# Moving one of three quantization passes over a weight tile from VectorE to ScalarE

## The chip, the cores and the metric

The kernel runs on all 8 cores of one Trainium2 chip. Each core works alone on its own rows: cores 2b and 2b+1 share batch b, and each owns every other block of 128 tokens of it, 2048 in all. The metric is the device time of one launch in microseconds, that of the slowest core, as a median over runs.

## The reference

One transformer layer in postnorm form on x of shape (4, 4096, 1024), float32: causal attention with 16 heads over a latent of 128, then a gated feed-forward block whose matrices and inputs are quantized.

```python
def _weight_quant(w):
    scale = 1.0 / jnp.clip(jnp.mean(jnp.abs(w)), 1e-05)
    wq = jnp.clip(jnp.round(w * scale), -1.0, 1.0) / scale
    return w + jax.lax.stop_gradient(wq - w)

def _act_quant(x):
    scale = 127.0 / jnp.clip(jnp.max(jnp.abs(x), axis=-1, keepdims=True), 1e-05)
    xq = jnp.clip(jnp.round(x * scale), -128.0, 127.0) / scale
    return x + jax.lax.stop_gradient(xq - x)

def _bitlinear(x, w):
    return jnp.einsum('bsi,oi->bso', _act_quant(x), _weight_quant(w))

# feed-forward: w_gate, w_up are (4096, 1024), w_down is (1024, 4096)
gate = jax.nn.silu(_bitlinear(x, w_gate))
up = _bitlinear(x, w_up)
ffn = _bitlinear(gate * up, w_down)

x = _layernorm(x + attention(x))
x = _layernorm(x + ffn(x))
```

What matters here is `_weight_quant`: each weight is multiplied by one scale, rounded, and clipped to -1, 0 or 1. The scale needs the mean over the whole matrix, so each matrix is read twice.

## The kernel before

Every instruction goes through `Prog.emit`, which appends it to the list of its engine with the semaphore counts that it waits for; each engine runs its list in that order. `set_auto` makes every VectorE, ScalarE and GpSimd instruction also wait for the one before it on its engine; DMAs are exempt from that. A DMA is issued by the engine on whose list it stands (SP, ScalarE or GpSimd), and it waits there for its own semaphores, so whatever stands behind it on that list waits as well.

The program has three blocks. The first computes keys, values and queries and, in between, quantizes the three feed-forward matrices; the second is attention with its output projection and layer norm; the third is the feed-forward block. The second and third are not touched.

In the first block a loop over `c5` (8 chunks of 512 tokens) transposes x (PE to PSUM, then copied out in turns by VectorE and ScalarE, L29 and L30), makes `kvT` (L396), and then runs 4 head groups `hc`. A head group is one long chain in which VectorE does nearly everything: L414 (copy out of PSUM) to L426, then `Ln` and `Exp` on ScalarE (L429, L432), then L435 to L492 on VectorE with short matmuls in between.

The quantization is a generator, `f0_emitter` (L260 to L331), of which `f0_step(n)` emits n steps at that place of every list. One step stands behind `kvT` and two behind each head group, nine in a chunk; `f0_step(200)` (L499) emits all that is left behind the last chunk. In the order of steps, for each of `wg` (8 tiles of 128x4096), `wu` (8 tiles of 128x4096) and `wd` (32 tiles of 128x1024):

- pass 1, one step a tile: load (L277), `Abs` with a row sum on ScalarE (L286), add on VectorE (L290);
- one step that turns the sum into the scale `sclw` (L294 to L300);
- pass 2, one step a tile: load (L310, DMA rows carry L311), then three instructions on VectorE: times scale plus MAGIC (L314, which rounds, MAGIC being 1.5*2^23), minus MAGIC and min 1 (L318), max -1 into bfloat16 (L322), then the store to DRAM (L325, L326).

There are two float32 buffers, `wfbuf[i % 2]`, but one bfloat16 buffer, since both entries of `wqbuf` are the same tile; so L322 waits until the store of the tile before has landed. Loads of even tiles are issued by SP, those of odd tiles by ScalarE. All stores are issued by SP, which makes its order: load of an even tile, its store, the store of the odd tile behind it, load of the next even tile. The load of tile i in pass 2 waits for the store of tile i-2:

```python
w = [(cV, mksc[1])]
if dmk[bi] is not None:
    w.append((qP[bi], dmk[bi][1]))
mkd = P.emit(y if bi == 0 else "scalar", ... dma_start(wfbuf[bi] <- src tile i), waits=w, ...)
```

By the counting of steps, pass 2 of `wg` has tile 0 behind `kvT` and then the pairs (1,2), (3,4), (5,6) behind head groups and tile 7 with the first tile of the next pass; pass 2 of `wu` has tiles 0 and 1 alone and then the pairs (2,3), (4,5), (6,7); pass 2 of `wd` has tile 0 alone, the pairs (1,2), (3,4), and the remaining 27 tiles (5 to 31) in one go with no other work between them: the drain.

Of the kernel before, what the change touches and what calls it, by code (L numbers as in the profile page):

```python
# [9 lines left out]
F32 = mybir.dt.float32  # L10
BF16 = mybir.dt.bfloat16
AF = mybir.ActivationFunctionType
ALU = mybir.AluOpType
# [76 lines left out]
def build_nc():  # L90
# [26 lines left out]
    with es:  # L117
# [17 lines left out]
        sclw = sb("sclw", [128, 1], F32)  # L135
        absacc = sb("absacc", [128, 1], F32)
        negMb = sb("negMb", [128, 1], F32)
        sm = sb("sm", [128, 16], F32)
        sm4 = sb("sm4", [4, 2048], F32)

# [16 lines left out]
        with at:  # L157
# [9 lines left out]
            with s1:  # L167
# [24 lines left out]
                with ps1:  # L192
# [15 lines left out]
                    def _gchain(fn):  # L208
                        global _unused
                        nonlocal _gprev  # L210
                        _gprev = P.emit(g, fn, waits=([_gprev] if _gprev else []), incs=[(cG, 1)])
                    _gchain(lambda e: e.memset(ident[:], 1.0))
                    _gchain(lambda e: e.affine_select(ident[:], ident[:], [[1, 128]], ALU.is_equal, 0.0, base=0, channel_multiplier=-1))
                    _gchain(lambda e: e.memset(mtmp[:], 1.0))
# [45 lines left out]
                    def f0_emitter():  # L260
                        dmk = [None, None]
                        for wi, (src, dst, nt, ncols) in enumerate(
                                [(dwg, sg, 8, INNER), (dwu, su, 8, INNER), (dwd, sd, 32, D)]
                                if STAGE >= 1 else []):
                            mk_z = P.emit(g, lambda e: e.memset(absacc[:], 0.0),
                                          waits=[(cV, cV.v)], incs=[(cG, 1)])
                            vmk = [None, None]
                            for i in range(nt):
                                bi = i % 2
                                w = [(cG, mk_z[1])] if i < 2 else []  # L270
                                if dmk[bi] is not None:
                                    w.append((qP[bi], dmk[bi][1]))
                                if vmk[bi] is not None:
                                    w.append((cV, vmk[bi][1]))
                                mkd = P.emit(y if bi == 0 else "scalar",
                                             lambda e, i=i, bi=bi, src=src, ncols=ncols:
                                             e.dma_start(out=wfbuf[bi][:, 0:ncols],  # L277
                                                         in_=src[i * 128:(i + 1) * 128, :]),
                                             waits=w, incs=[(qF[bi], 16)], dma=True)
                                wsm = [(qF[bi], mkd[1])]  # L280
                                wsm += [(qP[k], dmk[k][1]) for k in range(2) if dmk[k]]
                                if vmk[0] is not None:
                                    wsm.append(vmk[0])
                                if vmk[1] is not None:
                                    wsm.append(vmk[1])
                                mka = P.emit(s, lambda e, bi=bi, ncols=ncols: e.activation(  # L286
                                    wqbuf[bi][:, 0:ncols], wfbuf[bi][:, 0:ncols], AF.Abs,
                                    accum_out=sm[:, 0:1]), waits=wsm,
                                    incs=[(cA, 1)])
                                vmk[bi] = P.emit(v, lambda e: e.tensor_add(  # L290
                                    absacc[:], absacc[:], sm[:, 0:1]),
                                    waits=[(cA, mka[1])], incs=[(cV, 1)])
                                yield
                            mkmm = P.emit(t, lambda e: e.matmul(  # L294
                                ps_sw[:], onesf[:], absacc[:], start=True, stop=True),
                                waits=[(cV, cV.v)], incs=[(cT, 1)])
                            P.emit(v, lambda e, wi=wi: e.tensor_scalar(
                                swb[:, wi:wi + 1], ps_sw[:], 1.0 / float(INNER * D), 1e-5,
                                ALU.mult, ALU.max), waits=[(cT, mkmm[1])])
                            mksc = P.emit(v, lambda e, wi=wi: e.reciprocal(  # L300
                                sclw[:], swb[:, wi:wi + 1]), waits=[(cA, cA.v)],
                                incs=[(cV, 1)])
                            yield
                            for i in range(nt):
                                bi = i % 2
                                w = [(cV, mksc[1])]
                                if dmk[bi] is not None:
                                    w.append((qP[bi], dmk[bi][1]))
                                mkd = P.emit(y if bi == 0 else "scalar",
                                             lambda e, i=i, bi=bi, src=src, ncols=ncols:  # L310
                                             e.dma_start(out=wfbuf[bi][:, 0:ncols],  # L311
                                                         in_=src[i * 128:(i + 1) * 128, :]),
                                             waits=w, incs=[(qF[bi], 16)], dma=True)
                                P.emit(v, lambda e, bi=bi, ncols=ncols: e.tensor_scalar(  # L314
                                    wfbuf[bi][:, 0:ncols], wfbuf[bi][:, 0:ncols],
                                    sclw[:, 0:1], MAGIC, ALU.mult, ALU.add),
                                    waits=[(qF[bi], mkd[1])])
                                P.emit(v, lambda e, bi=bi, ncols=ncols: e.tensor_scalar(  # L318
                                    wfbuf[bi][:, 0:ncols], wfbuf[bi][:, 0:ncols],
                                    MAGIC, 1.0, ALU.subtract, ALU.min))  # L320
                                wv2 = [(qP[k], dmk[k][1]) for k in range(2) if dmk[k]]
                                vmq = P.emit(v, lambda e, bi=bi, ncols=ncols: e.tensor_scalar_max(  # L322
                                    wqbuf[bi][:, 0:ncols], wfbuf[bi][:, 0:ncols], -1.0),
                                    waits=wv2, incs=[(cV, 1)])
                                dmk[bi] = P.emit(y, lambda e, i=i, bi=bi, dst=dst, ncols=ncols:  # L325
                                                 e.dma_start(out=dst[i * 128:(i + 1) * 128, :],  # L326
                                                             in_=wqbuf[bi][:, 0:ncols]),
                                                 waits=[(cV, vmq[1])], incs=[(qP[bi], 16)])
                                yield
# [979 lines left out]
```

How the kernel before makes its waits and increments, by code:

```python
            def run(e):  # L74
                for fn, waits, incs in ops:
                    for h, v in waits:
                        e.wait_ge(h, v)
                    if fn is None:
                        assert not incs, "fn=None cannot carry incs"
                        continue
                    inst = fn(e)
                    for h, n in incs:
                        inst.then_inc(h, n)
```

## Time and profile before

| | us |
|---|---|
| median of 2 runs | 3676.5 (3674.17 to 3678.82) |
| the profiled execution | 3674.18 |
| span of its slowest core, core 0 | 3672.6 |
| spans of the 8 cores | 3645.8 to 3672.6 |
| mean granted TensorE clock of the cores | 0.635 to 0.694 of full speed |

| core 0, busy | us | share of the span |
|---|---|---|
| TensorE matmul | 1753.4 | 48% |
| VectorE | 1416.9 | 39% |
| ScalarE | 1014.3 | 28% |
| GpSimd | 18.8 | 1% |

| stage on core 0 | from, us | to, us |
|---|---|---|
| pass 2 of `wg`, between head groups | 163 | 326 |
| pass 2 of `wu`, between head groups | 445 | 572 |
| pass 2 of `wd`, tiles 0 to 4 | 894 | 950 |
| pass 2 of `wd`, the drain | 950 | 1083 |
| queries, attention, feed-forward | 1083 | 3673 |

A share of busy time is an average over stages with different limits; here each stage is read by itself. In the timeline a row is the start, the duration, the engine, the line, the operation, and in brackets how long the engine had been idle and what ended that. ACTq and SPq rows are DMA issues; several of one kind may be merged into one row ("x2").

### The profile page before, as it was taken

The numbers are of one execution on the slowest core, as the hardware profiler recorded it, in microseconds if no ns is written. First come the engines' busy times: TensorE is split into PE (matmuls) and PEld (weight loads), VectorE is DVE, ScalarE is ACT, GpSimd is POOL, SyncE is SP. The second block draws the span as 40 slices with busy tenths as digits, with TensorE's granted clock in tenths as the row PEclk, the third lists the DMA queues.
The fourth block names the chain that finished last, engine by engine and source line by source line (L and its number), as shares of the span: only waits on it lengthen the run. The fifth ranks groups of instructions, "written<-read, shape, count | busy, mean of one in ns | idle before, by whom it ended". The sixth has DMA issues, their size and how long they took to land.

```text
span 3672.6 us, 31765 instructions; the slowest of 8 cores (3645.8 to 3672.6 us)
## 1 busy us (share of the span) xinstructions
PE 1753.4 (48%) x8824; PEld 593.5 (16%) x8824; DVE 1416.9 (39%) x2757; ACT 1014.3 (28%) x1228; POOL 18.8 (1%) x54
## 2 busy tenths in 40 slices
PE   1201112222004443456577587719745862962874
PEld 0000000000001111111111111104312321421331
DVE  1453464444445554432321311144524524444352
ACT  1301301221000002457478488801201211120120
POOL 1000000000000000000000000000000000000000
PEclk9999555555555555555555555559977995986997
DMA  5445354221440000010100100033224223412522
GB/s 120 148 161 172 137 202 124 69 69 55 134 137 12 1 0 12 6 41 1 46 1 1 46 1 1 1 115 115 64 75 138 86 76 102 130 61 69 166 61 77
DMA packets 140977, 278.35 MB, mean 76 GB/s; under 512 B 7944, under 2 KB 106504, under 8 KB 134664
## 3 DMA queue, kind: packets, MB, share of 16 engines
q1 hardware_dynamic: 107256, 192.96, 15.9%
q10 hardware_dynamic: 24320, 67.12, 5.4%
q0 software_dynamic: 9232, 16.25, 2.8%
q8 instruction: 78, 1.28, 0.1%
q14 instruction: 91, 0.75, 0.1%
HBM read 250.61 MB, written 41.94 MB: 80 GB/s over the span
## 4 chain that ended last, share of the span: by engine, by line
PE 21%; ACT 16%; DVE 11%; DMA 7%; issue 4%; DVEq 1%; ACTq 0%; SPq 0%
PE ps_f L1063 6%; PE ps_f L1069 6%; PE ps_f L1177 5%; DMA wdbuf<-scr_d 4%; ACT PTb L730 4%; ACT PTb L734 4%; ACT PT L730 3%; ACT PT L734 3%; ACT hqT L30 2%; DMA xo_t<-xo 2%; DVE den_sb L808 1%; PE ps_sc L706 1%; DMA x1f<-scr_x 1%; DMA wubuf<-scr_u 1%; PE ps_den L761 1%
## 5 line engine op out<-in xcount | busy, mean ns | idle before, releaser
L706 PE MATMUL ps_sc<-qn,khat 32*128 32x512 bf16 (+3 forms) x1280 | 313.8, 531 | 136.3 <-ACT PT L730 50.1
L1177 PE MATMUL ps_f<-wdbuf,hqT 128*128 128x512 bf16 x1024 | 262.0, 406 | 97.2 <-DMA wdbuf<-scr_d 46.3
L1063 PE MATMUL ps_f<-wgbuf,xqT 128*128 128x512 bf16 x1024 | 248.6, 387 | 119.0 <-DMA wubuf<-scr_u 118.1
L1069 PE MATMUL ps_f<-wubuf,xqT 128*128 128x512 bf16 x1024 | 245.2, 383 | 0.0
L742 DVE TENSOR_TENSOR PT<-PT,maskD 128x512 bf16<-128x512 bf16 x64 | 27.2, 425 | 489.1 <-ACT PT L734 489.1
L1083 DVE SCALAR_TENSOR_TENSOR hbuf<-ps_f,xsc,gate_s 128x512 f32<-128x512 f32 x128 | 96.1, 751 | 273.5 <-ACT gate_s L1077 273.5
L730 ACT ACTIVATE PT<-ps_sc,negMb 128x1024 bf16<-128x1024 f32 (+3 forms) x160 | 157.8, 986 | 121.2 <-PE ps_sc L706 108.8
L1077 ACT ACTIVATE gate_s<-ps_f,xsc 128x512 f32<-128x512 f32 x128 | 88.0, 687 | 345.2 <-PE ps_f L1069 345.2
L353 PE MATMUL ps_tr<-ident,xst 128*128 128x128 bf16 x384 | 52.2, 304 | 268.0 <-DVE xTc L29 176.5
L286 ACT ACTIVATE wqbuf_s<-wfbuf 128x1024 bf16<-128x1024 f32 (+1 forms) x48 | 91.7, 1910 | 291.6 <-DVE absacc L290 127.7
L730 ACT ACTIVATE PTb<-ps_sc,negMb 128x1024 bf16<-128x1024 f32 (+3 forms) x160 | 157.8, 986 | 36.0 <-PE ps_sc L706 24.6
L734 ACT ACTIVATE PT<-ps_sc,negMb 128x1024 bf16<-128x1024 f32 (+3 forms) x160 | 157.8, 986 | 16.0 <-ACT PT L730 1.5
L734 ACT ACTIVATE PTb<-ps_sc,negMb 128x1024 bf16<-128x1024 f32 (+3 forms) x160 | 157.8, 986 | 14.8
L423 PE MATMUL ps_ss<-kr2buf,ind4T 128*4 128x512 bf16 x32 | 18.7, 585 | 298.8 <-DVE krall L418 298.8
L706 PEld LDWEIGHTS ps_sc<-qn,khat 32*128 32x128 bf16 x1280 | 69.5, 99 | 466.8 <-issue 465.5
L1063 PEld LDWEIGHTS ps_f<-wgbuf,xqT 128*128 128x128 bf16 x1024 | 101.1, 99 | 243.7 <-issue 127.4
L1177 PEld LDWEIGHTS ps_f<-wdbuf,hqT 128*128 128x128 bf16 x1024 | 98.0, 102 | 251.4 <-issue 170.5
L30 ACT COPY hqT<-ps_tf 128x512 bf16<-128x512 bf16 x128 | 75.1, 586 | 190.4 <-PE ps_tf L958 183.2
L429 ACT ACTIVATE sm<-sm 4x512 f32<-4x512 f32 x32 | 20.1, 628 | 376.4 <-DVE sm L426 376.4
L450 PE MATMUL ps_bc<-rkh,ind 4*128 4x512 bf16 x32 | 18.6, 580 | 217.3 <-DVE rkl L446 217.3
L1069 PEld LDWEIGHTS ps_f<-wubuf,xqT 128*128 128x128 bf16 x1024 | 101.3, 99 | 124.5 <-issue 6.6
L314 DVE TENSOR_SCALAR wfbuf<-wfbuf,sclw 128x1024 f32<-128x1024 f32 (+1 forms) x48 | 61.7, 1286 | 120.9 <-DMA wfbuf<-wdT 74.8
(223 smaller groups left out, 2403.2 us busy)
## 6 DMA issues: line engine op xcount, KB each, us to landing
wgbuf<-scr_g SPq DMA_DIRECT2D x32, 1024.0 KB, 5.5
wubuf<-scr_u SPq DMA_DIRECT2D x32, 1024.0 KB, 8.4
wfbuf<-wgT SPq DMA_DIRECT2D x8, 2048.0 KB, 10.5
wfbuf<-wgT ACTq DMA_DIRECT2D x8, 2048.0 KB, 9.1
wfbuf<-wuT SPq DMA_DIRECT2D x8, 2048.0 KB, 14.0
wfbuf<-wuT ACTq DMA_DIRECT2D x8, 2048.0 KB, 10.3
wfbuf<-wdT SPq DMA_DIRECT2D x32, 512.0 KB, 3.8
wfbuf<-wdT ACTq DMA_DIRECT2D x32, 512.0 KB, 3.9
```

Of the source, the lines that this page charges most:

```text
L30: return e.copy(dst, src)
L286: mka = P.emit(s, lambda e, bi=bi, ncols=ncols: e.activation(wqbuf[bi][:, 0:ncols], wfbuf[bi][:, 0:ncols], AF.Abs, accum_out=sm[:, 0:1]), ...
L314: P.emit(v, lambda e, bi=bi, ncols=ncols: e.tensor_scalar(wfbuf[bi][:, 0:ncols], wfbuf[bi][:, 0:ncols], sclw[:, 0:1], MAGIC, ALU.mult, ALU ...
L353: e.transpose(ps_tr[bank][:, i4 * 128:(i4 + 1) * 128], src, ident[:]),
L706: e.matmul(ps_sc[:, j * 512 + stc:j * 512 + 512], khat[32 * j:32 * j + 32, gi * T + sc * 128: gi * T + sc * 128 + 128], qn[32 * j:32 * j + 32,
L730: mk_expA = P.emit(s, lambda e, stc=stc, pp=pp: e.activation(PTr[pp][:, 0:2, stc:512], PSr[:, 0:2, stc:512], AF.Exp, bias=negMb[:, 0:1]), ...
L734: mk_exp = P.emit(s, lambda e, stc=stc, pp=pp: e.activation(PTr[pp][:, 2:4, stc:512], PSr[:, 2:4, stc:512], AF.Exp, bias=negMb[:, 0:1]), w ...
L1063: P.emit(t, lambda e, c=c, i4=i4, bi=bi, gb=gb: e.matmul(ps_f[:, gb:gb + 512], xqT[:, i4 * D + c * 128:i4 * D + c * 128 + 128], wgbuf[bi][ ...
L1069: P.emit(t, lambda e, c=c, i4=i4, bi=bi, ub=ub: e.matmul(ps_f[:, ub:ub + 512], xqT[:, i4 * D + c * 128:i4 * D + c * 128 + 128], wubuf[bi][ ...
L1077: e.activation(gate_s2[par][:], ps_f[:, gb:gb + 512], AF.Silu, scale=xsc[:, c8 + 3:c8 + 4]),
L1083: e.scalar_tensor_tensor(hbuf[:, i4 * INNER + io * 512: i4 * INNER + io * 512 + 512], ps_f[:, ub:ub + 512], xsc[:, c8 + 4:c8 + 5], gate_s2 ...
L1177: e.matmul(ps_f[:, ((2 + i4) % 4) * 512: ((2 + i4) % 4) * 512 + 512], hqT[:, i4 * INNER + io * 128: i4 * INNER + io * 128 + 128], wdbuf[bi ...
```

## The change

In pass 2 the multiplication by the scale and the addition of MAGIC become one `activation` with `AF.Identity` on ScalarE, in place on the float32 tile, with `sclw` as its scale and a new constant tile `magicc` as its bias, both read from a column of 128 values. VectorE keeps L318 and L322. The activation waits for the load; L318 waits for the activation. The load of tile i no longer waits for the store of tile i-2 but for L322 of that tile (for the first two tiles of a matrix the old wait stays). GpSimd sets `magicc` once at the start. The list of ScalarE in pass 2 becomes: activation of an even tile, load of the odd tile behind it, activation of that tile.

```diff
--- before.py
+++ after.py
@@ -135,6 +135,7 @@
         sclw = sb("sclw", [128, 1], F32)
         absacc = sb("absacc", [128, 1], F32)
         negMb = sb("negMb", [128, 1], F32)
+        magicc = sb("magicc", [128, 1], F32)
         sm = sb("sm", [128, 16], F32)
         sm4 = sb("sm4", [4, 2048], F32)
 
@@ -209,6 +210,7 @@
                         global _unused
                         nonlocal _gprev
                         _gprev = P.emit(g, fn, waits=([_gprev] if _gprev else []), incs=[(cG, 1)])
+                    _gchain(lambda e: e.memset(magicc[:], MAGIC))
                     _gchain(lambda e: e.memset(ident[:], 1.0))
                     _gchain(lambda e: e.affine_select(ident[:], ident[:], [[1, 128]], ALU.is_equal, 0.0, base=0, channel_multiplier=-1))
                     _gchain(lambda e: e.memset(mtmp[:], 1.0))
@@ -301,27 +303,38 @@
                                 sclw[:], swb[:, wi:wi + 1]), waits=[(cA, cA.v)],
                                 incs=[(cV, 1)])
                             yield
+                            vmq2 = [None, None]
                             for i in range(nt):
                                 bi = i % 2
                                 w = [(cV, mksc[1])]
-                                if dmk[bi] is not None:
+                                if vmq2[bi] is not None:
+                                    w.append(vmq2[bi])
+                                elif dmk[bi] is not None:
                                     w.append((qP[bi], dmk[bi][1]))
                                 mkd = P.emit(y if bi == 0 else "scalar",
                                              lambda e, i=i, bi=bi, src=src, ncols=ncols:
                                              e.dma_start(out=wfbuf[bi][:, 0:ncols],
                                                          in_=src[i * 128:(i + 1) * 128, :]),
                                              waits=w, incs=[(qF[bi], 16)], dma=True)
+                                wA = [(qF[bi], mkd[1]), (cV, mksc[1])]
+                                if vmq2[bi] is not None:
+                                    wA.append(vmq2[bi])
+                                mka2 = P.emit(s, lambda e, bi=bi, ncols=ncols:
+                                              e.activation(
+                                                  wfbuf[bi][:, 0:ncols],
+                                                  wfbuf[bi][:, 0:ncols], AF.Identity,
+                                                  bias=magicc[:, 0:1],
+                                                  scale=sclw[:, 0:1]),
+                                              waits=wA, incs=[(cA, 1)])
                                 P.emit(v, lambda e, bi=bi, ncols=ncols: e.tensor_scalar(
                                     wfbuf[bi][:, 0:ncols], wfbuf[bi][:, 0:ncols],
-                                    sclw[:, 0:1], MAGIC, ALU.mult, ALU.add),
-                                    waits=[(qF[bi], mkd[1])])
-                                P.emit(v, lambda e, bi=bi, ncols=ncols: e.tensor_scalar(
-                                    wfbuf[bi][:, 0:ncols], wfbuf[bi][:, 0:ncols],
-                                    MAGIC, 1.0, ALU.subtract, ALU.min))
+                                    MAGIC, 1.0, ALU.subtract, ALU.min),
+                                    waits=[(cA, mka2[1])])
                                 wv2 = [(qP[k], dmk[k][1]) for k in range(2) if dmk[k]]
                                 vmq = P.emit(v, lambda e, bi=bi, ncols=ncols: e.tensor_scalar_max(
                                     wqbuf[bi][:, 0:ncols], wfbuf[bi][:, 0:ncols], -1.0),
                                     waits=wv2, incs=[(cV, 1)])
+                                vmq2[bi] = (cV, vmq[1])
                                 dmk[bi] = P.emit(y, lambda e, i=i, bi=bi, dst=dst, ncols=ncols:
                                                  e.dma_start(out=dst[i * 128:(i + 1) * 128, :],
                                                              in_=wqbuf[bi][:, 0:ncols]),
```

## Rows read from the trace of the kernel before

**Rows 1.** Busy us of each engine in the drain of `wd`.

```profile
core 0: us, PE busy (x) PEld busy (x) DVE busy (x) ACT busy (x) POOL busy (x), PEclk, DMA share, GB/s
...
950.00:1083.00 133.00, 0.00 (x0) 0.00 (x0) 58.30 (x83) 0.59 (x1) 0.00 (x0) 0.50 0.48 156
```

**Rows 2.** Groups of instructions by line, VectorE, 0 to 1100 us, shapes kept apart.

```profile
L314 DVE TENSOR_SCALAR wfbuf<-wfbuf,sclw 128x4096 f32<-128x4096 f32 x16 | 37.6, 2353 | 44.9 <-DMA wfbuf<-wgT 32.4 <-DMA wfbuf<-wuT 11.4
...
L314 DVE TENSOR_SCALAR wfbuf<-wfbuf,sclw 128x1024 f32<-128x1024 f32 x32 | 24.1, 753 | 76.0 <-DMA wfbuf<-wdT 74.8
```

**Rows 3.** Groups of instructions by line, ScalarE, whole span, shapes kept apart.

```profile
L730 ACT ACTIVATE PT<-ps_sc,negMb 128x1024 bf16<-128x1024 f32 x112 | 124.8, 1114 | 92.5 <-PE ps_sc L706 84.5 <-ACT PTb L734 0.3
...
L286 ACT ACTIVATE wqbuf_s<-wfbuf 128x4096 bf16<-128x4096 f32 x16 | 57.9, 3616 | 126.4 <-DMA wfbuf<-wgT 57.1 <-DMA wfbuf<-wuT 45.2 <-DVE absacc L290 23.9
L286 ACT ACTIVATE wqbuf_s<-wfbuf 128x1024 bf16<-128x1024 f32 x32 | 33.8, 1056 | 165.1 <-DVE absacc L290 103.9 <-DMA wfbuf<-wdT 49.9 <-DVE rkh L445 10.8
```

**Rows 4.** Timeline around a tile pair of `wg` (start us, duration us, engine, line).

```profile
226.55 0.63 ACT L432 ACTIVATE sm<-sm 4x512 f32<-4x512 f32 x1
226.67 0.33 ACTq L311 DMA_DIRECT2D wfbuf<-wgT  x1
227.35 0.68 DVE L435 TENSOR_TENSOR sm<-sm 4x512 f32<-4x512 f32 x1 [1.67 <-ACT sm L432]
...
238.45 2.35 DVE L314 TENSOR_SCALAR wfbuf<-wfbuf,sclw 128x4096 f32<-128x4096 f32 x1
...
246.15 0.33 SPq L311 DMA_DIRECT2D wfbuf<-wgT  x1
255.95 2.35 DVE L314 TENSOR_SCALAR wfbuf<-wfbuf,sclw 128x4096 f32<-128x4096 f32 x1 [10.35 <-DMA wfbuf<-wgT]
258.41 2.29 DVE L318 TENSOR_SCALAR wfbuf<-wfbuf 128x4096 f32<-128x4096 f32 x1
```

**Rows 5.** Timeline around a tile pair of `wu`.

```profile
511.05 0.69 DVE L414 CAST krbuf<-ps_a 128x512 bf16<-128x512 f32 x1
511.53 0.33 SPq L311 DMA_DIRECT2D wfbuf<-wuT  x1
...
526.67 2.35 DVE L314 TENSOR_SCALAR wfbuf<-wfbuf,sclw 128x4096 f32<-128x4096 f32 x1
...
541.19 0.69 DVE L414 CAST krbuf<-ps_b 128x512 bf16<-128x512 f32 x1
```

**Rows 6.** Timeline of the drain of `wd`: one pair, and the last load on SP.

```profile
953.91 0.33 SPq L311 DMA_DIRECT2D wfbuf<-wdT  x1
...
957.80 0.75 DVE L314 TENSOR_SCALAR wfbuf<-wfbuf,sclw 128x1024 f32<-128x1024 f32 x1 [4.44 <-DMA wfbuf<-wdT]
...
962.45 0.69 DVE L322 TENSOR_SCALAR wqbuf_s<-wfbuf 128x1024 bf16<-128x1024 f32 x1 [0.34 <-DMA scr_d<-wqbuf_s]
963.69 0.33 SPq L311 DMA_DIRECT2D wfbuf<-wdT  x1
...
1073.25 0.33 SPq L311 DMA_DIRECT2D wfbuf<-wdT  x1
```

**Rows 7.** Timeline, ScalarE and its DMA queue around 864 us, an earlier pass.

```profile
863.94 1.06 ACT L286 ACTIVATE wqbuf_s<-wfbuf 128x1024 bf16<-128x1024 f32 x1
...
864.09 0.33 ACTq L277 DMA_DIRECT2D wfbuf<-wdT  x1
```

**Rows 8.** Landing of L311 loads issued at 226.67, 246.15, 904.5, and all from 950 us.

```profile
DMA to landing us min/median/max: 8.1/8.1/8.1
...
DMA to landing us min/median/max: 9.6/9.6/9.6
...
DMA to landing us min/median/max: 3.4/3.4/3.4
...
DMA to landing us min/median/max: 3.6/4.1/5.1
```

**Rows 9.** Timeline, one small memset on GpSimd.

```profile
9.83 0.09 POOL L235 MEMSET kmax<- 4x4 f32 x1 [0.18 <-POOL c L234]
```

## The prediction, made before the change was run

> **What bounds the kernel now.** I first asked for the busy time of the engines in stretches, to see which stages the change can touch: only pass 2 of the three matrices, in the first 1083 us. Then the groups by line give the price of one instruction, and the timeline of the three passes shows who waits for whom. In the drain of `wd` VectorE works 58.3 of 133 us and ScalarE almost nothing [rows 1], so no engine is full: each pair of tiles is a chain of latencies. A load on SP is issued at 953.91, VectorE starts on the tile at 957.80, and the next load on SP goes out at 963.69, behind the store of the odd tile [rows 6]. From 953.91 to 1073.25 there are 12 such periods, 9.945 us each. In `wg` the odd tile is ready when VectorE comes to it (238.45), and the even tile behind it is waited for: its load is issued at 246.15, after the odd tile's store, and VectorE starts at 255.95 [rows 4]. In `wu` the pairs are the other way round (even, odd) and both loads land while the head group's chain runs: from 511.05 to 541.19 VectorE hardly waits [rows 5].
>
> **The change, part by part.** It removes L314 from VectorE: 16 of 2.353 and 32 of 0.753 us, 61.7 us in all [rows 2]; with the 0.11 us to the next instruction (from 255.95 + 2.35 to 258.41, [rows 4]) 2.46 and 0.86 us a tile. What is left on VectorE is 4.69 us for a large tile (2 x 2.29 + 0.11, [rows 4]) and 1.49 us for a small one (2 x 0.69 + 0.11, [rows 6]).
>
> It adds 48 ACTIVATEs with two column operands. The trace has none like that. `Abs` without one takes 1.056 us for 1024 columns and 3.616 for 4096; `Exp` with one column (the bias) takes 1.114 for 1024 [rows 3]. I take 1.11 and 3.67 (3.62 plus the same 0.06); the low end is 1.06 and 3.62. From the end of an activation to the VectorE instruction that waits for it pass 0.17 us (226.55 + 0.63 to 227.35, [rows 4]). From the landing of a load (246.15 + 9.6, [rows 8]) to the start of the waiting instruction pass 0.2 us [rows 4]. What the second column costs no row shows. The Trainium skill (ScalarE: Activation LUTs, What ACT_TABLE_LOAD costs) states 186 ns plus 0.833 ns a column and about 93 ns for each column operand, 1.22 us here; the first column costs only 0.06 in this trace, so I stay at the row, and by the page the sum below would be about 4 us more.
>
> So a tile whose load VectorE has to wait for loses 3.67 + 0.17 - 2.46 = 1.38 us (large) or 1.11 + 0.17 - 0.86 = 0.42 us (small). A tile whose activation is over in time gains 2.46 or 0.86.
>
> The order on ScalarE's list is what decides. The load of an odd tile now stands behind the activation of the even tile before it, and that waits for the even load. Before, it only stood behind `Exp` and the store of two tiles ago. That it need not wait for the end of the activation is shown at 863.94: an ACTIVATE of 1.06 us starts, and the DMA behind it is issued 0.15 us later [rows 7]. Behind the activations wait `Ln` of the next head group and the copies L30. Both need VectorE's work of after the tiles, so the activations, ended before it, cost them nothing; if an odd activation ended after L318 and L322 of its tile could have, that is already counted as VectorE's wait. On SP nothing moves: the even load stands behind the odd store, later than either of its waits, so dropping the wait for the store gives nothing there.
>
> *wg.* Odd tile: its load is issued at 226.67 behind `Exp`, lands 8.1 us later [rows 8], the activation runs from 234.97 to 238.64, VectorE can start at 238.81 in place of 238.45: gain 2.46 - 0.36 = 2.10. Even tile: +1.38. Three pairs are -0.72 each, tile 0 is waited for (+1.38), tile 7 is odd (-2.10): -2.9 in all.
>
> *wu.* Tiles 0 and 1 are waited for: +2.8. A pair, counted from L414 (511.05): even load issued at 0.48, ready at 10.28 if it takes the 9.80 us of the same kind of load in `wg` (246.15 to 255.95: one store and no other load beside it), its activation over at 13.95. VectorE is free at 15.62 (526.67) and does its two instructions until 20.31. The odd load is issued at 10.43 and takes 8.1 + 0.2: activation from 18.73 to 22.40, VectorE from 22.57 to 27.26, next L414 at 27.37 in place of 30.14 [rows 4, 5, 8]. Three pairs gain 2.77 each: -8.3, with the first two tiles -5.5. If the odd load took 2.8 us longer the gain would be gone; that is the other bound.
>
> *wd, tiles 0 to 3.* Tiles 0 and 2 are waited for, 1 and 3 are not: 2 x 0.42 - 2 x 0.86 = -0.9.
>
> *wd, the drain.* Tile 4 and the 27 behind it make 14 pairs. Load on SP to ready 3.89 (953.91 to 957.80, [rows 6]); the odd load is issued 0.15 later [rows 7]; it lands 3.4 us after its issue when alone and 4.1 in the median of the present drain, where two loads overlap [rows 8]. Now only a store joins it near its end, so I take 3.5, with 0.2 to the start; activation 1.11, to VectorE 0.17, two instructions 1.49, and 0.55 from the end of L322 to the next load on SP (962.45 + 0.69 to 963.69, [rows 6]). Sum 3.89 + 0.15 + 3.70 + 1.11 + 0.17 + 1.49 + 0.55 = 11.06 against 9.945: 1.115 more, 14 times, **+15.6 us**. The even tile's activation lies inside this (the odd load runs beside it); the wait of L322 for the store (0.34 before 962.45) vanishes in it too. Bounds: the odd load at 3.4 and the activation at 1.06 give +13.5; both loads at 4.1 + 0.2 give a period of 12.07 and +29.8.
>
> *GpSimd.* One more memset ahead of the loads of the weights: 0.09 + 0.18 [rows 9], +0.3.
>
> **Sum:** -2.9 - 5.5 - 0.9 + 15.6 + 0.3 = +6.6 us on the profiled 3674.2, that is 3680.8. That execution lies 2.3 below the median of the two runs, so I say 3676.5 + 6.6 = **3683 us**. About 2% (73 us) is what a measurement of this kernel can tell from no change; all my terms together are far inside. Nothing behind 1083 us is touched; it comes later by the sum. The cores span 3645.8 to 3672.6 us with clocks from 0.635 to 0.694, not in the same order, so a few us may come from there as well.
>
> **Rivals.**
> 1. *The loads of the drain land no faster than now* (4.1 us each). For it: the 8 cores read at the same time. Against it: the 3.4 of a load alone. Drain +29.8, total +20.8: 3697. Chance 0.15.
> 2. *The place of the odd load costs nothing.* Then it is ready when VectorE comes to it: 3.89 + 1.11 + 0.17 + 1.49 = 6.66, L322 of the odd tile waits for the store until 2.3 later (960.15 to 962.45), +0.69 + 0.55 = 10.2: +0.26 a pair, +3.6, total -5.4: 3671. Against it: ScalarE's list is in order, and 11.06 follows from that. The Trainium skill (DMA: Bandwidth & Descriptors, Issuing engines are not separate DMA queues) says that issuing from several engines saves only the time to initiate a DMA. This rival is that rule read strictly; it leaves out what the issuing engine waits for first. Chance 0.06.
> 3. *VectorE's saving comes out whole*, as it would if VectorE were the bound in every stage: -61.7, 3615. Against it: the idle time before L314 at 255.95 and 957.80 [rows 4, 6]. Chance 0.04.
> 4. *The odd load waits for the end of the activation*: some 1.0 more in 14 pairs and 3.5 in three: +25 over my sum, 3707. Against it: [rows 7]. Chance 0.06.
> 5. *Slower beyond 2%: writing float32 in place runs at half ScalarE's pace*, 1.96 and 7.1 us. No row has Identity from SBUF in place at this size. Drain +0.85 x 28 = 24, `wg` 8 x 3.4 = 27, `wu` some 17 (tiles 0, 1 and three pairs, 3.4 each): 68 over my sum, 3751. It decides from about 2 us for a small tile. Against it: column count alone explains every row of [rows 3]. Chance 0.03.
>
> My forecast has 0.62; 0.04 is left for what I don't see. The range **3670 to 3698** takes in my forecast's bounds, rivals 1 and 2: 0.83. Forecast alone: 3676 to 3690. Faster by over 2%: 0.01 (even rival 3 is 1.7%). Slower by over 2%: 0.03 and a little, 0.04. Within: 0.95.
>
> **What the changed profile would show.** The ACTIVATE at about 1.11 and 3.67 us; L318 idle before it, ended by ScalarE, in all even tiles and in the odd ones of the drain; the period between loads on SP in the drain at 11.1 us in place of 9.9; the odd load issued 0.15 us after the even activation's start; the period of a `wu` pair at 27.4 in place of 30.1; the drain about 150 us long. It would be wrong if the odd loads go out earlier than that, if a load alone on the queue needs more than 4 us, or if `Ln` or L30 wait for an activation.

## The result and the profile after

The changed kernel takes 3704.1 us (median of 11 runs) against 3675.3 us before (10 runs): ratio 1.0082, 95% interval 1.0056 to 1.0107, that is 21 to 39 us slower. The forecast was 3683 with a range to 3698; the time lies outside it. Its profiled execution has a span of 3700.5 us on its slowest core, core 5, where `wg` is longer too (169.9 us, 162.0 before); its last store of `wd` is issued 29.8 us after that of the latest core before (1116.4 against 1086.5 us).

The time went in the place that was named, but more of it. The table gives the mean of the 8 cores in the two profiled executions; a stage runs from the issue of its first load in pass 2 to that of its last store, and "between" is what lies between two such stages. The pair is the mean over the SP loads in the last 118 us before that last store.

| stage, us | before | after | difference | forecast |
|---|---|---|---|---|
| pass 2 of `wg` | 162.1 | 165.1 | +3.0 | -2.9 |
| between | 118.7 | 119.3 | +0.5 | 0 |
| pass 2 of `wu` | 127.3 | 124.2 | -3.0 | -5.5 |
| between | 321.5 | 319.7 | -1.8 | 0 |
| pass 2 of `wd` | 191.1 | 215.8 | +24.6 | +14.7 |
| one pair in the drain (SP load to SP load) | 10.05 | 11.96 | +1.91 | +1.12 |
| last store of `wd` issued at | 1080.3 | 1102.9 | +22.6 | +6.6 |
| from there to the end | 2582.1 | 2583.9 | +1.8 | 0 |

The new instruction, by line and shape (busy us, mean ns):

```profile
L323 ACT ACTIVATE wfbuf<-wfbuf,magicc,sclw 128x4096 f32<-128x4096 f32 x16 | 60.8, 3800 | 154.3 <-DMA wfbuf<-wgT 73.2 <-DMA wfbuf<-wuT 57.9 <-DVE kmax L484 8.8
...
L323 ACT ACTIVATE wfbuf<-wfbuf,magicc,sclw 128x1024 f32<-128x1024 f32 x32 | 39.7, 1240 | 175.9 <-DMA wfbuf<-wdT 168.7 <-DVE rkh L458 7.2
```

It takes 1.24 and 3.80 us, where 1.11 and 3.67 were taken from [rows 3]. The VectorE instructions left are as before, 0.69 and 2.29 us. One pair of the drain on core 5, to be read beside [rows 6]:

```profile
971.86 0.33 SPq L316 DMA_DIRECT2D wfbuf<-wdT  x1
975.78 1.24 ACT L323 ACTIVATE wfbuf<-wfbuf,magicc,sclw 128x1024 f32<-128x1024 f32 x1 [6.14 <-DMA wfbuf<-wdT]
975.91 0.33 ACTq L316 DMA_DIRECT2D wfbuf<-wdT  x1
977.20 0.69 DVE L329 TENSOR_SCALAR wfbuf<-wfbuf 128x1024 f32<-128x1024 f32 x1 [5.88 <-ACT wfbuf L323]
978.00 0.69 DVE L334 TENSOR_SCALAR wqbuf_s<-wfbuf 128x1024 bf16<-128x1024 f32 x1
...
980.04 1.24 ACT L323 ACTIVATE wfbuf<-wfbuf,magicc,sclw 128x1024 f32<-128x1024 f32 x1 [3.01 <-DMA wfbuf<-wdT]
981.45 0.69 DVE L329 TENSOR_SCALAR wfbuf<-wfbuf 128x1024 f32<-128x1024 f32 x1 [2.76 <-ACT wfbuf L323]
982.25 0.69 DVE L334 TENSOR_SCALAR wqbuf_s<-wfbuf 128x1024 bf16<-128x1024 f32 x1
983.49 0.65 SPq L316 DMA_DIRECT2D wfbuf<-wdT  x1
```

Load on SP at 971.86, activation at 975.78; the odd load goes out 0.13 us later, behind it on ScalarE's list, and only when the even load has landed. Its own activation starts at 980.04, 4.13 us on. From there 1.24 and 0.17 to L329 (the old L318), two instructions until 982.94 (L334 is the old L322), and 0.55 to the next load. Each load is now waited for in full, one after the other. The drain as a whole on that core, in the columns of [rows 1]:

```profile
core 5: us, PE busy (x) PEld busy (x) DVE busy (x) ACT busy (x) POOL busy (x), PEclk, DMA share, GB/s
...
950.00:1116.00 166.00, 0.00 (x0) 0.00 (x0) 38.58 (x56) 35.29 (x29) 0.00 (x0) 0.50 0.40 129
```

VectorE works 38.6 of 166 us, where it worked 58.3 of 133 on core 0 before. Taking work from it gave only idle time.

A pair of `wu` on the same core, beside [rows 5]:

```profile
520.94 0.69 DVE L427 CAST krbuf<-ps_a 128x512 bf16<-128x512 f32 x1
521.41 0.33 SPq L316 DMA_DIRECT2D wfbuf<-wuT  x1
...
533.23 3.80 ACT L323 ACTIVATE wfbuf<-wfbuf,magicc,sclw 128x4096 f32<-128x4096 f32 x1 [7.59 <-DMA wfbuf<-wuT]
533.35 0.33 ACTq L316 DMA_DIRECT2D wfbuf<-wuT  x1
...
541.75 3.80 ACT L323 ACTIVATE wfbuf<-wfbuf,magicc,sclw 128x4096 f32<-128x4096 f32 x1 [4.72 <-DMA wfbuf<-wuT]
...
545.72 2.29 DVE L329 TENSOR_SCALAR wfbuf<-wfbuf 128x4096 f32<-128x4096 f32 x1 [3.83 <-ACT wfbuf L323]
...
550.52 0.69 DVE L427 CAST krbuf<-ps_b 128x512 bf16<-128x512 f32 x1
```

From L427 (the old L414) at 520.94 to the next at 550.52 it is 29.6 us, against 30.1 before. The even load, issued at 521.41, was ready only at 533.23, 11.8 us later, and the odd one (533.35) at 541.75. The order is as worked out; the even load took 2 us more than the 9.8 that I carried over from `wg`, so little of the 2.8 us gain is left in this pair.

### The profile page after: what moved, and what is told of

Same layout as the page of the kernel before. It is cut to its first block, busy times and chain, and to the rows that moved or that the text cites. A ratio compares the mean times of both kernels' runs of the same rounds, so it can differ in the third digit from the quotient of the medians.

```text
span 3700.5 us, 31906 instructions; the slowest of 8 cores (3673.5 to 3700.5 us)
## 1 busy us (share of the span) xinstructions
PE 1749.2 (47%) x8824; PEld 593.4 (16%) x8824; DVE 1354.8 (37%) x2709; ACT 1114.7 (30%) x1276; POOL 18.8 (1%) x55
## 4 chain that ended last, share of the span: by engine, by line
PE 20%; ACT 15%; DVE 11%; DMA 7%; issue 5%; DVEq 1%; ACTq 0%; SPq 0%
PE ps_f L1076 6%; PE ps_f L1082 6%; PE ps_f L1190 5%; DMA wdbuf<-scr_d 4%; ACT PTb L747 4%; ACT PTb L743 4%; ACT PT L743 3%; ACT PT L747 3%; ACT hqT L30 2%; DMA xo_t<-xo 1%; DVE den_sb L821 1%; PE ps_sc L719 1%; DMA x1f<-scr_x 1%; DMA wubuf<-scr_u 1%; PE ps_den L774 1%
## 5 line engine op out<-in xcount | busy, mean ns | idle before, releaser
L323 ACT ACTIVATE wfbuf<-wfbuf,magicc,sclw 128x1024 f32<-128x1024 f32 (+1 forms) x48 | 100.5, 2093 | 330.2 <-DMA wfbuf<-wdT 168.7
L329 DVE TENSOR_SCALAR wfbuf<-wfbuf 128x1024 f32<-128x1024 f32 (+1 forms) x48 | 58.9, 1227 | 231.0 <-ACT wfbuf L323 230.6
## 6 DMA issues: line engine op xcount, KB each, us to landing
wfbuf<-wgT SPq DMA_DIRECT2D x8, 2048.0 KB, 10.3
```

Source lines behind the costliest of these rows:

```text
L323: e.activation(wfbuf[bi][:, 0:ncols], wfbuf[bi][:, 0:ncols], AF.Identity, bias=magicc[:, 0:1], scale=sclw[:, 0:1]),
L329: P.emit(v, lambda e, bi=bi, ncols=ncols: e.tensor_scalar(wfbuf[bi][:, 0:ncols], wfbuf[bi][:, 0:ncols], MAGIC, 1.0, ALU.subtract, ALU.min) ...
```

## The experiments

Stage figures below are means of the 8 cores of one profiled execution, taken as in the table. All ratios are to the kernel before on the same chip.

### Which stage carries the loss

The activation on ScalarE for tiles 4 to 31 of `wd` alone, and then for `wg` and `wu` alone:

```diff
-    <activation on ScalarE, then L329>
+    if wi == 2 and i >= 4:      # second kernel: if wi < 2:
+        <activation on ScalarE, then L329>
+    else:
+        <the three VectorE instructions of before>
```

> The activation on ScalarE only for tiles 4 to 31 of wd; wg, wu and the first tiles of wd keep the three VectorE instructions. Theory: the drain alone carries the loss: period 11.95 against 10.08 us, 14 pairs, 26 us, ratio 1.007. Rival: what was seen as longer between head groups (wg 3 us longer in the mean of the cores, up to 11 on one core) carries much of it; then the ratio is 1.004 or less.

Measured: 3705.5 us, ratio 1.0096 (1.0065 to 1.0126); drain period 12.07, `wd` 217.0, `wg` 162.2, `wu` 127.1. The drain alone makes the loss. The profiled execution took 3732 us, and the part behind `wd` was 2594 us in it in the mean of the cores (2582 to 2588 in the other profiles), longer on four cores that run the same instructions there; why is open. One more of the six runs was above 3726, the other four lie at 3701 to 3706, so the median does not rest on these two.

> The complement: the activation on ScalarE for wg and wu only, wd as before. By the profile of the changed kernel wg is 3.0 us longer and wu 3.0 us shorter in the mean of the cores: ratio 1.000, within 0.2%. By the prediction's own terms, with the activation at 3.80 instead of 3.67 us, about 6 us faster, ratio 0.998. Rival: ScalarE waiting for loads delays the head groups, ratio over 1.003.

Measured: 3691.5 us, ratio 1.0035 (1.0021 to 1.0049), outside both of my expectations. The rival had such a ratio, but not for this reason: `wg` 163.9 and `wu` 124.9 are near the values after, and it is `wd` that took 203.6, not 191.1, with a period of 11.01, though its three passes all ran on VectorE again. One thing was not as before in it: the new wait of the loads. That was not foreseen.

### The wait that was dropped

First the changed kernel with the old wait, a run set up together with the two above:

```diff
-    if vmq2[bi] is not None:
-        w.append(vmq2[bi])
-    elif dmk[bi] is not None:
+    if dmk[bi] is not None:
         w.append((qP[bi], dmk[bi][1]))
```

> The changed kernel with the old wait: the load of tile i waits for the store of tile i-2 again, and nothing else is changed. Both theories above: no load is issued later than in the changed kernel, since each stands behind something later on its list, so the time is that of the changed kernel, ratio to before about 1.007, drain period 11.9 to 12.1 us. Rival: loads released earlier collide with the stores and are what costs; then it goes back toward the kernel before, ratio under 1.003.

Measured: 3703.4 us, ratio 1.0073 (1.0049 to 1.0097), period 12.00. In the changed kernel the wait makes no difference, as expected. Then, made for what the run on `wg` and `wu` had shown, the kernel before with the new wait and nothing else:

> The kernel before (all three passes on VectorE) with only the new wait: a load waits for L322 of the tile two before, not for that tile's store. Theory of pacing: the store's wait held the odd load back by 1.7 us, behind the even load, which is needed first; without it the odd load is issued 0.5 us ahead of the even one, which then lands in 4.8 us instead of 3.9, and the drain's period is 11.0 us instead of 10.05: 13 us in 14 pairs, ratio to before 1.0035. Rival: the 11.0 seen with ScalarE on wg and wu only came from something else in that kernel; then this one equals the kernel before, ratio within 0.1%.

Measured: 3693.3 us, ratio 1.0034 (1.0018 to 1.0049), period 11.14, `wd` 205.3 (191.1 before). The theory of pacing holds. The timeline of its drain on core 0:

```profile
1016.46 0.69 DVE L343 TENSOR_SCALAR wqbuf_s<-wfbuf 128x1024 bf16<-128x1024 f32 x1 [0.63 <-DMA scr_d<-wqbuf_s]
1017.23 11.99 ACTq L316 DMA_DIRECT2D wfbuf<-wdT  x2
1017.70 0.33 SPq L316 DMA_DIRECT2D wfbuf<-wdT  x1
1022.83 0.75 DVE L335 TENSOR_SCALAR wfbuf<-wfbuf,sclw 128x1024 f32<-128x1024 f32 x1 [5.68 <-DMA wfbuf<-wdT]
```

The odd load (ACTq, 1017.23; the row merges two issues) now leaves 0.5 us ahead of the even load (SPq, 1017.70), which VectorE needs first, and the even tile is ready 5.1 us after its issue in place of 3.9 [rows 6]. In the median the even load lands after 4.9 us and the odd one after 4.1; before it was 3.9 and 4.6. Waiting for the store had held the less urgent load back.

### Order or length

Two causes were left for the 1.9 us a pair: the odd load's place behind the activation, and the activations' own length. First only the place was changed:

```diff
+    if i + 1 < nt and (i + 1) % 2 == 1:
+        ld2[i + 1] = load2(i + 1)    # ahead of the activation of tile i
     <activation of tile i>
```

> The changed kernel, but the load of an odd tile is issued before the activation of the even tile ahead of it instead of behind it; the work of every engine is the same. Theory of order (the odd load waits on ScalarE's list until the even load has landed): the two loads overlap again, the drain's period falls from 11.95 us (mean of the 8 cores) to about 10.7, 17 us less in 14 pairs, and the odd tiles of wg, whose activation ends about 2 us late, are ready in time, some 8 us less: about 25 us below the changed kernel, about 3680, ratio to before 1.001. Rival theory of length (the activations themselves, 1.24 and 3.80 us plus 0.17 to VectorE, lengthen the chain, whatever the order): it stays within 5 us of the changed kernel, ratio 1.006 or more.

Measured: 3717.4 us, ratio 1.0114 (1.0084 to 1.0145): slower than the changed kernel, against both theories. Period 11.71, and `wg` 178.0 in place of 165.1. The drain on core 0, and a pair of `wg` on core 5:

```profile
1020.68 0.37 ACTq L319 DMA_DIRECT2D wfbuf<-wdT  x1
1021.49 0.33 SPq L319 DMA_DIRECT2D wfbuf<-wdT  x1
1026.78 2.58 ACT L331 ACTIVATE wfbuf<-wfbuf,magicc,sclw 128x1024 f32<-128x1024 f32 x2 [9.53 <-DMA wfbuf<-wdT]
1028.19 0.69 DVE L337 TENSOR_SCALAR wfbuf<-wfbuf 128x1024 f32<-128x1024 f32 x1 [7.60 <-ACT wfbuf L331]
```

```profile
241.71 0.32 SPq L347 DMA_DIRECT2D scr_g<-wqbuf_s  x1
241.72 0.35 ACTq L319 DMA_DIRECT2D wfbuf<-wgT  x1
242.18 0.33 SPq L319 DMA_DIRECT2D wfbuf<-wgT  x1
259.76 3.80 ACT L331 ACTIVATE wfbuf<-wfbuf,magicc,sclw 128x4096 f32<-128x4096 f32 x1 [29.84 <-DMA wfbuf<-wgT]
```

It is the finding of the last section once more: the odd load leaves ahead of the even one. In the drain the even load is ready only 5.3 us after its issue; in `wg`, where a store of 1 MB, the odd load and the even load, 2 MB each, leave in this order within 0.5 us, 17.6 us after it, and VectorE waits for just that load. So this run did not separate the theories. The next keeps the odd load ahead of the activation, but with the wait for the store, and in `wd` only:

> The changed kernel, in wd only: the odd load ahead of the even tile's activation, and waiting again for the store of two tiles ago, as in the kernel before. Theory of order: with the odd load neither behind the activation nor ahead of the even load, the drain's period is about 10.6 us (even ready at 4.1, activations to 5.3 and about 7.7, L322 of the odd tile held by the store until 9.3) against 11.96, 19 us less than the changed kernel in 14 pairs; ratio to before about 1.002. Theory of length: the two activations on the chain cost the same wherever the load is issued, the period stays above 11.5, ratio about 1.006.

Measured: 3690.9 us, ratio 1.0028 (1.0013 to 1.0042), period 10.74, `wd` 200.2; 15.6 us of the drain's loss are gone with the same instructions on every engine. A pair on core 0:

```profile
1005.56 0.33 SPq L319 DMA_DIRECT2D wfbuf<-wdT  x1
1007.30 0.33 ACTq L319 DMA_DIRECT2D wfbuf<-wdT  x1
1009.54 1.24 ACT L331 ACTIVATE wfbuf<-wfbuf,magicc,sclw 128x1024 f32<-128x1024 f32 x1 [6.94 <-DMA wfbuf<-wdT]
1010.95 0.69 DVE L337 TENSOR_SCALAR wfbuf<-wfbuf 128x1024 f32<-128x1024 f32 x1 [5.94 <-ACT wfbuf L331]
1011.75 0.69 DVE L342 TENSOR_SCALAR wqbuf_s<-wfbuf 128x1024 bf16<-128x1024 f32 x1
1012.21 1.24 ACT L331 ACTIVATE wfbuf<-wfbuf,magicc,sclw 128x1024 f32<-128x1024 f32 x1 [1.43 <-DMA wfbuf<-wdT]
...
1013.62 0.69 DVE L337 TENSOR_SCALAR wfbuf<-wfbuf 128x1024 f32<-128x1024 f32 x1 [1.17 <-ACT wfbuf L331]
1014.76 0.70 DVE L342 TENSOR_SCALAR wqbuf_s<-wfbuf 128x1024 bf16<-128x1024 f32 x1 [0.45 <-DMA scr_d<-wqbuf_s]
1016.35 0.33 SPq L319 DMA_DIRECT2D wfbuf<-wdT  x1
```

Load on SP at 1005.56, odd load 1.7 us behind it, both activations over by 1013.45; what sets the end is, as before the change, the odd tile's L342, held for the store of the even one. The theory of order holds for the larger part: of 1.91 us a pair, 1.22 (11.96 to 10.74) are the place behind the activation (the old wait, which came back with it, had changed nothing by itself in the changed kernel) and 0.69 (to 10.05) the longer chain. The chain can be read too: in the last 12 pairs of each core, from the landing of the even load to the end of that tile's L342 it is 3.19 us in the mean, where it was 2.55 before to the end of L322, because the activation and the step to VectorE stand in place of the shorter L314.

The length of the activation was tried by itself:

```diff
-    bias=magicc[:, 0:1], scale=sclw[:, 0:1]
+    bias=0.0, scale=1.0
```

> The changed kernel with the activation's scale 1.0 and bias 0.0 as constants in place of the two column operands; this leaves out the scaling and rounding of the weights. If the columns are what makes the activation 1.24 and 3.80 us, they take 1.06 and 3.62 as Abs does, and the drain's period falls by 0.36 us to 11.6 (5 us in 14 pairs). Rival: writing float32 in place costs it; then the durations stay at 1.24 and 3.80.

Measured: 3689.1 us in one run, period 11.84, and

```profile
L323 ACT ACTIVATE wfbuf<-wfbuf 128x4096 f32<-128x4096 f32 x16 | 57.9, 3618 | 139.8 <-DMA wfbuf<-wgT 79.3 <-DMA wfbuf<-wuT 60.5
...
L323 ACT ACTIVATE wfbuf<-wfbuf 128x1024 f32<-128x1024 f32 x32 | 33.8, 1057 | 179.1 <-DMA wfbuf<-wdT 175.4 <-DVE rkh L457 3.7
```

The two columns cost 0.18 us an activation at both sizes, and writing float32 in place costs nothing beside `Abs` (1.06 and 3.62 [rows 3]). The period fell by 0.12 only, not by 0.36. The expectation had counted both activations of a pair, but only that of the odd tile stands on the chain: 0.18. The even loads took 0.09 us longer in the mean of the last 12 pairs (4.03 against 3.94), which leaves the 0.1 measured. The 3689.1 us themselves are one run; `wg` was 6 us shorter in it than after, and that is not explained.

### What the order of loads is worth

If pass 2 is bound by loads that are issued late, the cure is to issue them early. Both loads stand one tile ahead, first with the activation on ScalarE, then with all passes on VectorE:

```diff
+    if i + 1 < nt:
+        ld2[i + 1] = load2(i + 1)    # load of tile i+1 ahead of work and store of tile i
```

> The changed kernel with both loads issued one tile ahead: the load of tile i+1 stands ahead of the activation of tile i, and on SP ahead of the store of tile i, so that no tile is waited for in wg, and two loads fly in the drain. If latency of loads is what bounds pass 2: wg 35 us less, wu 12 less, the drain's period 7.5 to 8.1 us, some 55 us less, and VectorE's saved 2.46 us in each large tile comes out: about 100 us under the changed kernel, ratio to before about 0.975. Rival: bandwidth (loads and stores collide, as with the odd load alone ahead) takes most of it; ratio over 0.99.

Measured: 3616.6 us, ratio 0.983 (0.9805 to 0.9855); `wg` 136.9, `wu` 120.8, `wd` 162.6, period 8.3.

> The same order of loads with all three passes on VectorE. Drain period 6.8 to 7.6 us by latency, 45 us less than before; wg 40, wu 12 us less than before; ratio about 0.975. Against the run with ScalarE in the same order: with the loads out of the way VectorE is the bound between head groups, so ScalarE's version should be up to 39 us faster there (16 x 2.46) and some 8 us slower in the drain. If the two are equal within 0.3%, moving the pass to ScalarE is worth nothing even then.

Measured: 3639.5 us, ratio 0.9886 (0.9867 to 0.9904); `wg` 146.3, `wu` 129.8, `wd` 163.0, period 8.2. Both gain less than expected. In `wg` a new wait stands where the old one was:

```profile
202.40 0.36 ACTq L319 DMA_DIRECT2D wfbuf<-wgT  x1
202.43 2.35 DVE L343 TENSOR_SCALAR wfbuf<-wfbuf,sclw 128x4096 f32<-128x4096 f32 x1
204.88 2.29 DVE L347 TENSOR_SCALAR wfbuf<-wfbuf 128x4096 f32<-128x4096 f32 x1
212.24 2.29 DVE L351 TENSOR_SCALAR wqbuf_s<-wfbuf 128x4096 bf16<-128x4096 f32 x1 [5.06 <-DMA scr_g<-wqbuf_s]
```

The odd load (ACTq, 202.40) now flies together with the store issued at that moment, and L351 (the old L322) of the next tile, writing the single bfloat16 buffer, waits 5.1 us for that store. In this order the pass on ScalarE is worth something: 9.5 us in `wg` and 9.0 in `wu`, and nothing in the drain.

The buffers are sized for 4096 columns and a tile of `wd` has 1024, so for `wd` each of them can hold several:

```diff
+    ns = 4 if wi == 2 else 2
+    wf = wfbuf[k % 2][:, 1024 * (k // 2):...]     # k = i % ns
+    wq = wqbuf_s[:, 1024 * k:...] if wi == 2 else wqbuf_s
+    wait of L322's successor: the store of tile i-4, not of the tile before
```

> All three passes on VectorE, loads ahead, and for wd four slots of 1024 columns in the same buffers (for the float32 tile and for the bfloat16 one), so that three loads fly and the store of four tiles ago is waited for. If latency and the single bfloat16 buffer bound the drain (period 8.2 us a pair with one tile ahead): VectorE then sets it at 2.5 us a tile, 5 us a pair, 45 us less, ratio to before about 0.977. If bandwidth does: 1.5 MB a pair at the 160 to 200 GB/s seen so far are 7.7 to 9.5 us, no gain over 0.9886.

> The same with the first pass on ScalarE. Between head groups it keeps the 20 us that ScalarE's version was ahead with one tile ahead; in the drain ScalarE needs 1.4 and VectorE 1.6 us a tile, 3.2 a pair, so bandwidth must be the bound: if the version on VectorE reached 5 us a pair this one is at most a little better there. Ratio about 0.97. If bandwidth bounds both at 7.7 or more, ratio 0.982, as without the slots.

Measured: 3587.6 us, ratio 0.9754 (0.9737 to 0.977), with VectorE alone, and 3574.5 us, ratio 0.9721 (0.970 to 0.9741), with ScalarE: 2.8% faster than before, the fastest of all. `wd` takes 115.5 and 119.5 us. The drain on core 0, VectorE alone and then with ScalarE:

```profile
core 0: us, PE busy (x) PEld busy (x) DVE busy (x) ACT busy (x) POOL busy (x), PEclk, DMA share, GB/s
926.00:981.00 55.00, 0.00 (x0) 0.00 (x0) 47.62 (x67) 0.58 (x1) 0.00 (x0) 0.50 0.94 314
```

```profile
901.00:956.00 55.00, 0.00 (x0) 0.00 (x0) 29.62 (x43) 26.95 (x22) 0.00 (x0) 0.50 0.92 298
```

In the first VectorE works 47.6 of 55 us, with 0.11 us between its instructions: only now is it the bound, 4.9 us a pair. In the second it works 29.6 of 55, and yet a pair takes 5.15 us on this core. The DMA engines are busy 92% of the time there, but they moved less than in the first (298 against 314 GB/s), so their share does not make them the bound. The timeline of the second shows what does:

```profile
935.73 0.69 DVE L354 TENSOR_SCALAR wqbuf_s<-wfbuf 128x1024 bf16<-128x1024 f32 x1
...
936.50 0.35 ACTq L332 DMA_DIRECT2D wfbuf<-wdT  x1
937.06 2.58 ACT L342 ACTIVATE wfbuf<-wfbuf,magicc,sclw 128x1024 f32<-128x1024 f32 x2 [2.58 <-DVE wqbuf_s L354]
938.48 0.69 DVE L347 TENSOR_SCALAR wfbuf<-wfbuf 128x1024 f32<-128x1024 f32 x1 [2.06 <-ACT wfbuf L342]
...
940.88 0.69 DVE L354 TENSOR_SCALAR wqbuf_s<-wfbuf 128x1024 bf16<-128x1024 f32 x1
...
941.65 0.35 ACTq L332 DMA_DIRECT2D wfbuf<-wdT  x1
942.21 2.57 ACT L342 ACTIVATE wfbuf<-wfbuf,magicc,sclw 128x1024 f32<-128x1024 f32 x2 [2.58 <-DVE wqbuf_s L354]
```

It is ScalarE's list once more. The load of an odd tile stands there ahead of an activation and waits for L354 (the old L322) of the tile whose slot it takes, so the activation behind it waits for VectorE as well, though its own tile has landed: the first activation and the step to VectorE 1.42 us (937.06 to 938.48), four VectorE instructions 3.09, 0.08 to the load, 0.56 from its issue to the next activation, 5.15 in all. Of the 88 activations of the even tiles 8 to 28 on the 8 cores, 77 start 0.3 to 3.0 us after their own load has landed, 11 as soon as it lands. What the drain would take with the odd loads off ScalarE's list, no run shows. My fear of 160 to 200 GB/s as a limit was wrong, and the whole advantage of ScalarE's version, 13 us, comes from `wg` and `wu` (17 us there, less 4 in `wd`).

## Why the prediction was wrong

- **That the drain decides, and in which way: right.** The odd load leaves 0.13 us after the start of the even activation (0.15 forecast), the period grows, VectorE's saving is not on the path there. Placing the odd load elsewhere gave back 15.6 us. What failed is the size.
- **How long the two loads of a drain pair take: the step that failed.** For the odd load I took 3.5 us from [rows 8], near a lone load of 3.4. That was one load on one core. The same lone load (L311 on ScalarE's queue, ahead of the drain) on core 1 of the same execution:

```profile
DMA to landing us min/median/max: 4.0/4.0/4.0
```

  Over the 8 cores and both such loads it lands in 3.4 to 4.1 us, 3.8 in the mean. In the drain after, its median is 3.7 on the even-numbered cores and 4.0 on the odd-numbered ones. The even load's 3.89 came from one period of core 0. The terms of a pair, beside the mean of the last 12 pairs of each core:

| term of a pair, us | forecast | measured |
|---|---|---|
| even load, from issue to the start of its activation | 3.89 | 4.21 |
| to the issue of the odd load | 0.15 | 0.13 |
| odd load, from issue to the start of its activation | 3.70 | 4.13 |
| activation | 1.11 | 1.24 |
| to VectorE | 0.17 | 0.17 |
| two VectorE instructions | 1.49 | 1.49 |
| to the next load on SP | 0.55 | 0.57 |
| sum | 11.06 | 11.94 |

  The loads land after 3.94 and 3.86 us in the mean, and from landing to the start of an activation it is 0.27 us, not the 0.2 taken from VectorE's row. The two loads are 0.75 of the 0.88 us that were missing in each pair, the activation is 0.13.
- **Rival 1** (the loads land no faster than now) had just this price, +29.8 us in the drain; the cores' mean is 14 x 1.91 = 26.7. I gave it 0.15 because of the one row with 3.4. Its total, 3697, is still 7 us short of the measured time: it kept my gain of 8.4 us in `wg` and `wu`, and in this profile the two together gained nothing.
- **The activation: mis-sized.** 1.24 and 3.80 in place of 1.11 and 3.67, 0.13 more; one of the two lies on the chain of a pair, since the odd load runs beside the other. By the Trainium skill (ScalarE: Activation LUTs, What ACT_TABLE_LOAD costs) it would be 1.22 and 3.78, an estimate from the page's figures; the trace agrees with the page to 0.02 us. The row I preferred had one column and read PSUM.
- **Rival 2** (the place of the odd load costs nothing, a pair of 10.2 us) is ruled out: with the odd load issued ahead of that activation, and with the same work, a pair is 1.22 us shorter (11.96 to 10.74).
- **wu: right in mechanism, smaller in size**, -3.0 for -5.5: the even load was slower than in `wg`. In the four other profiles with the activation there and this order of loads `wu` took 123.4 to 126.8 us, in the three without it 127.1 to 127.7.
- **wg: the gain is not settled.** With the activation in this order of loads it took 165.1, 161.3, 163.9, 164.4 and 158.8 us (the last without the columns), with VectorE alone 162.1, 162.2 and 161.8. In three of these five profiles two neighbouring cores have 170 to 172 us there and the others 159 to 167; with VectorE alone no core was above 167. On those pairs of cores all even loads behind the first land late, in 10.3 to 12.6 us; elsewhere most of the later ones land in 9.1 to 9.6. Why, no run shows. Where all three landed within 9.6 us, `wg` took 160.4 us in the mean of six cores with VectorE alone and 159.6 in that of nine with the activation (columns included): a gain of 0.8, not the 2.9 forecast.
- **"Dropping the wait gives nothing": right for the changed kernel, wrong as a reason.** I looked only at whether the old wait ended last. It also set which load leaves first, and without it the kernel before loses 11 us in the medians and 14 in `wd`.
- Core 0, on which all rows were read, had the least loss of all (+7.8 us at the end of `wd`; the mean is 22.6). Its two profiles differ already at the first load of `wg` (163.4 and 155.9 us), so this is partly chance between executions.

## What to carry to other kernels

When work moves to an engine that also issues loads, read that engine's list as a queue: a load behind an instruction that waits for another load turns two overlapping transfers into two in sequence. Before dropping a wait, ask not only whether it ends last but which transfer it keeps behind which. And where an engine is busy less than half of a stage, early loads and more buffers come first: the same move of work lost 29 us in the old order of loads and gained 13 to 23 in the new one. A price for a transfer is to be read on all cores: one row of one core was 0.4 us too low here, in each of 14 pairs.

## What the runs showed of the hardware

A load of 512 KB with nothing else of its core in flight takes 3.4 to 4.1 us here (before, ahead of the drain), with seven other cores at work; of two that overlap, issued 1.7 us apart, the first takes 3.9 and the second 4.6 in the median. So two overlapping loads are over 6.3 us after the first issue, and two in sequence only after some 8.

Of transfers issued within 0.5 us of each other the first also landed first, and the last one late. In the drain, 3.9 us became 4.9 for the even load behind the odd one. In `wg`, a 2 MB load issued 0.5 us behind a 1 MB store and another 2 MB load took 14.6 to 17.7 us (odd load ahead of the activation), where it takes 9.1 to 11.2 behind the store alone (before). A 1 MB store issued within 0.1 us of a 2 MB load landed after 9.3 to 10.7 us (both loads one tile ahead), in place of 3.8 to 5.3 with nothing beside it or an even load 0.4 us behind it.

A load that waits on ScalarE's list holds up the activation behind it, even one whose data has landed (2.58 us idle in the last timeline). Small tiles with three loads in flight, with their stores, reached 314 GB/s on core 0, twice the 156 of the old drain.
